# A fused 16-batch transformer and scan kernel: the transfers that stack Q and K's second half, divided by head groups and waited for one batch later

## The reference

```python
x = x + attention(layernorm(x), Wqkv, Wproj)      # 16 heads of 16, rotary, causal softmax
x = x + quant_linear(layernorm(x), weight, bias)  # blocks of 32 rounded to an fp6 grid
x = x + mamba_block(layernorm(x), ...)            # in_proj, conv, scan over 1024 steps, MLP
x = x + quant_linear(layernorm(x), weight, bias)
```

## Time and profile before

| | us |
|---|---|
| median of 3 runs | 10044.25 |
| lowest and highest | 10041.67, 10044.95 |
| profiled execution | 10042.81 |
| its span, first to last instruction | 10040.9 |
| TensorE busy | 7867.1 (78%) |
| VectorE busy | 7696.5 (77%) |
| ScalarE, GpSimd busy | 4309.5, 4340.3 (43% each) |

### The profile page before, as it was taken

One profiled execution on the slowest core, in us unless ns is written; L12 is line 12 of the kernel. 1 busy time (PEld: TensorE's weight loads), 2 busy tenths in 40 slices (PEclk: granted clock), 3 DMA queues, 4 the chain that ended last, 5 costly groups with the idle time before them and its releaser, 6 DMA issues. The chain is left out here.

```text
span 10040.9 us, 98208 instructions
## 1 busy us (share of the span) xinstructions
PE 7867.1 (78%) x31796; PEld 3819.5 (38%) x31796; DVE 7696.5 (77%) x11686; ACT 4309.5 (43%) x8247; POOL 4340.3 (43%) x2663
## 2 busy tenths in 40 slices
PE   5787787787877878787887878778787787877877
PEld 2343343433434334343343433434343343432434
DVE  4787877779687686876868768787787877878777
ACT  2534535354442543525435254353534535345352
POOL 1451714518154171542716336262361724517145
PEclk8898988989889898888989889898898988989889
DMA  3010020200202002020020200102011020100202
GB/s 76 1 38 15 5 48 1 51 1 5 48 0 51 1 9 44 0 51 1 12 40 0 51 1 21 32 0 52 1 28 25 0 52 1 38 15 5 48 0 51
DMA packets 260295, 229.91 MB, mean 23 GB/s; under 512 B 22051, under 2 KB 232739, under 8 KB 259635
## 3 DMA queue, kind: packets, MB, share of 16 engines
q1 hardware_dynamic: 259782, 223.48, 11.6%
HBM read 151.60 MB, written 70.25 MB: 22 GB/s over the span
## 5 line engine op out<-in xcount | busy, mean ns | idle before, releaser
L625 POOL TENSOR_TENSOR arena<-arena 128x1024 f32<-128x1024 f32 x1024 | 2434.3, 2387 | 1330.6 <-DVE arena L1007 879.0
L766 ACT ACTIVATE PS<-arena,Aneg 128x512 f32<-128x512 f32 x2048 | 1410.6, 691 | 1627.2 <-DVE XNT L1047 883.2
L690 ACT ACTIVATE arena<-PS 128x512 f32<-128x512 f32 (+3 forms) x3072 | 1286.8, 509 | 867.0 <-PE PS L1213 861.8
L914 DVE TENSOR_REDUCE pm<-PS 128x1 f32<-128x512 f32 (+3 forms) x1728 | 1050.6, 661 | 336.5 <-PE PS L1192 234.9
L1327 PE MATMUL PS<-XNT,identf 128*128 128x512 f32 x2048 | 1012.1, 618 | 320.0 <-POOL XNT L608 320.0
L587 POOL TENSOR_SCALAR_AFFINE_SELECT arena<-arena 128x512 f32<-128x512 f32 x512 | 328.2, 641 | 2114.5 <-ACT arena L690 2114.5
L1189 PE MATMUL PS<-arena 96*128 96x512 bf16 (+3 forms) x3072 | 1098.0, 382 | 178.8 <-PEq L1411 87.3
L1327 PE MATMUL PS<-arena,identf 128*128 128x512 f32 x2048 | 1025.5, 624 | 161.8 <-DVE arena L1023 161.8
L1213 PE MATMUL PS<-arena 99*128 99x512 bf16 (+3 forms) x3072 | 891.8, 331 | 5.4
L1150 PE MATMUL PS<-identf,arena 128*128 128x128 f32 x1280 | 284.1, 387 | 776.0 <-POOL arena L577 664.6
L1312 PE MATMUL PS<-arena,sel 96*128 96x512 bf16 x1664 | 513.4, 391 | 389.2 <-DVE arena L1023 319.7
(11 more groups left out here) (140 smaller groups left out, 13240.7 us busy)
## 6 DMA issues: line engine op xcount, KB each, us to landing
pieces_scratch<-arena SPq DMA_DIRECT2D x816, 64.0 KB
arena<-pieces_scratch SPq DMA_DIRECT2D x34, 768.0 KB
arena<-pieces_scratch SPq DMA_DIRECT2D x51, 512.0 KB
arena<-pieces_scratch SPq DMA_DIRECT2D x17, 1536.0 KB
arena<-in_x SPq DMA_DIRECT2D x17, 1024.0 KB, 5.6
U<-in_x SPq DMA_DIRECT2D x17, 1024.0 KB, 5.6
arena<-pieces_scratch SPq DMA_DIRECT2D x17, 1024.0 KB
out<-X SPq DMA_DIRECT2D x64, 256.0 KB, 8.3
```

Of the source, the lines that this page charges most:

```text
L625: nc.gpsimd.tensor_tensor(DB[:, n % 2], DTU[:, j, half(th)].unsqueeze(1).to_broadcast([P, SP2, TH]), BB[:, SP2 * sg:SP2 * (sg + 1), :], AL ...
L690: A(PT[s % len(PT)][:, hh, 0:w], bank(t_bank(n))[:, 0:w], ACT.Exp, scale=DH ** -0.5)\
L766: A(bank(da_bank(m)), DT[:, j, half(th)], ACT.Exp, scale=Aneg[:, j, SP2 * sg + ss:SP2 * sg + ss + 1]).then_inc(S("dA"), 1)
L914: V_.tensor_reduce(out=dst, in_=bank(r % 3)[:, 0:share * w].rearrange("p (h w) -> p h w", h=share), op=ALU.max, axis=AX.X, negate=True).th ...
```

## The change

`stack` takes the semaphore that its commands raise. There are four new semaphores, `stacked[0..3]`, one for each group of four heads. K's first half is stacked as before. K's second half and Q are stacked group by group (K, then Q, three commands each), which makes 24 commands out of 6. SP's wait for `pj` stands behind the K commands of group 0. SP no longer waits for these transfers at the end of a pass; PE waits for group g ahead of that group's first score unit in the next pass. In each pass SP, after its twelve maxima commands, waits for each group's semaphore and sets it to zero. The block behind the loop waits for the four as well.

```diff
+        stacked = [ctx.enter_context(nc.semaphore(f"stacked_{g}")) for g in range(NG)]
...
-        def stack(sp, qk, heads, cols):
+        def stack(sp, qk, heads, cols, done):
...
-                  .then_inc(S("stack"), 16)
+                  .then_inc(done, 16)
...
-        N_STACK = 1 + 3 * len(RUNS[0])
+        N_STACK = 1 + len(RUNS[1])
+        N_GROUP = 16 * (len(RUNS[0]) + len(RUNS[1]))
...
-            stack(sp, 1, ALL, half(0))
+            stack(sp, 1, ALL, half(0), S("stack"))
             store_pieces(sp, 2)
             store_pieces(sp, 3)
             sp.wait_ge(S("pcd"), N_PCD * NT // 2)
-            stack(sp, 1, ALL, half(1))
-            if in_loop:
-                sp.wait_ge(S("pj"), NT * 3)
-            stack(sp, 0, ALL, slice(0, T))
+            for g in range(NG):
+                heads = slice(g * HG, (g + 1) * HG)
+                stack(sp, 1, heads, half(1), stacked[g])
+                if in_loop and g == 0:
+                    sp.wait_ge(S("pj"), NT * 3)
+                stack(sp, 0, heads, slice(0, T), stacked[g])
...
+            for g in range(NG):
+                sp.wait_ge(stacked[g], N_GROUP)
+                sp.sem_clear(stacked[g])
             sp.wait_ge(S("dB"), NM)
...
+                    if u % NS1 == 0:
+                        pe.wait_ge(stacked[g], N_GROUP)
                     if r >= 3 and not at:
                         pe.wait_ge(S("red"), r - 2)
...
                 sp.wait_ge(landed, N_OUT)
+                for g in range(NG):
+                    sp.wait_ge(stacked[g], N_GROUP)
```

## The result

| | before | changed |
|---|---|---|
| median, us | 10044.21 | 9967.47 |
| profiled execution, us | 10042.81 | 9965.80 |
| its span, us | 10040.9 | 9963.4 |

The ratio is 0.9924, with a 95% interval of 0.9913 to 0.9936. (The medians are over six runs each; one run of the changed kernel, at a mean granted clock of 0.65, is far above the others and left out of the ratio.)

The account below looks back on a forecast made before the run. SP, waiting for the stack's last bytes, was taken to bound each pass's end; 40.7 + 21.6 - 1.5 = 60.8 us gained gave 9983.4 against 10044.25 (0.61% faster), own range 9976 to 9995, stated range 9974 to 9998.

Parts of the forecast that it names:

- The bound: At a pass's end, SP and behind it the stack's last bytes are the last arrival at the barrier.
- Ahead of the loop: SP leaves after issuing 24 commands, taken as 12 us, at 132.3 instead of 154.0: gain 21.6, range 18 to 26.
- 15 x 2.71: Removing SP's mean end-of-pass wait of 2.71 us at 15 boundaries gains 40.7 us, one for one.
- The check at two boundaries: Boundary waits of 3.9 and 2.3 us: 1.6 more wait, 2.7 longer pass; "the size allows one for one".
- The transfers themselves. Same bytes, same row length: Stack transfers as 24 commands take up to 10% (3.4 us) longer, covered by 20 us: cost nothing.
- The sign that the wait for output would grow to 3.4 us: At the head of each pass, the wait for output grows from 0.7 to about 3.4 us if right.
- I take 0, as the bytes and rows are the same: End of the kernel: one wait falls away, SP's last output wait grows equally; no gain, 0 to 3 lost.
- The added waits: PE's four waits a pass, 64 in all, and SP's waits and clearings cost 1.5 us, range 0.8 to 6.4.
- A: 24 commands hold SP, slower: 10051 at 1.36 us each, turning at 1.33; chance 0.03 above 1.39, 0.04 shared with full B below.
- B: Gain given back behind the barrier to output traffic: 10044, or 10023 if only boundaries fail; in part 0.06, in full within 0.04.
- C: The wait moves from SP to PE, which must wait for group 0; ahead of the loop 9986; chance 0.01.
- The range: Own range 9976 to 9995 from prologue, waits, tail and run-to-run terms; widened to 9974 to 9998 for boundary jitter.

## Why the prediction was wrong, point by point

- **The bound** was read rightly: SP with the stack's last bytes was the last arrival at the barrier, and from SP's last arrival to PE's first load there are 2.3 us in both kernels.
- **Ahead of the loop**: 21.6 forecast, 22.2 measured. SP was held 11.3 us for the 24 commands (12 taken), and PE didn't wait.
- **"15 x 2.71"**, a wait that passes into the time one for one, is the mis-sized term that put the time below the range: 3.39 a pass and 50.9 in all, some 10 of the 16 us missing. The boundary itself gave 2.6 a pass; the other 0.8 came from stages that weren't changed, 1.4 from the attention, where the granted clock falls elsewhere, less 0.6 that the stages behind it took back. The experiments show that lengths of passes don't add up here (0.8 us later at a boundary costs nothing, 1.8 costs 3.4); why they settle where they do stays open. The check at two boundaries gave a warning that was passed over: 1.6 more wait had gone with 2.7 more pass. The pass behind the long wait had another clock than the one before it, at the same place:

```profile
4000.76:4010.76 10.00, 7.85 (x54) 6.44 (x51) 3.46 (x10) 2.77 (x5) 0.27 (x1) 1.00 0.01 2
```

  1.00 where the pass from 3243.77 had 0.83. "The size allows one for one" should have been "it doesn't".
- **"The transfers themselves. Same bytes, same row length"** is the step whose mechanism was wrong. It put a price of 0 to +10% on the division and never asked whether it could be negative, though the rows of before had a hint: 127 GB/s in Q's first command and 200 in its second, at the same row length (the view of the first boundary shows both). The stack became 8 us faster in the mean. In the loop the number didn't suffer by it, as the wait is gone in either way; as far as this step goes, that is luck. The sign that the wait for output would grow to 3.4 us failed by it: that wait is gone. And it was wrong at the end, where "I take 0, as the bytes and rows are the same" stood: behind SP's last command 3.3 us were gained.
- **The added waits** (1.5) can't be found; their cost is below what the passes show.
- **Rivals.** A: 24 commands took 11.3 to 12.9 us, some 0.5 each, far from 1.33. B: the gap behind SP's last command is unchanged, and no output traffic is left by then. C: PE didn't wait for group 0. The cost that the Trainium skill ("DMA: Bandwidth & Descriptors", section "Anatomy of one DMA") gives each transfer, about 2.0 us, overlaps here: 24 commands landed within 24 us at the first boundary, sooner than the six. Its advice in "Measured (HBM→SBUF...)", batches of 1 MiB or more, isn't borne out here: commands of 64 to 384 KB moved at 183 GB/s in the mean, those of 256 to 1536 KB at 139. The page gives both for transfers that GpSimd issues; those here are SP's.
- **The range** was built on bounds of terms that were seen. Some 10 of the 16 us missing come from a term that had no bounds at all, the stages that weren't changed.

## What to carry to other kernels

Before a wait is moved, ask whether the thing waited for can be made faster: here the division alone emptied the wait, and only the unhidden part ahead of the loop needed the move. A division of a transfer into 24 commands took it from 34 us to 26 or to 73 at the same bytes and row lengths, so it belongs in the sum with both signs. Read such a duration at many passes: one boundary had it at 24.0 where the trace has 23.7 to 27.6. In a loop whose passes are bound by TensorE in part, a microsecond saved or added at one end isn't a microsecond of time: look at the granted clock at the same place of the pass in both kernels before a small gain is put down to the edit.

## What the hardware showed that wasn't expected

- A pass stays at 614.4 us with 2.2 us saved or 0.8 us lost ahead of the next pass, and goes to 617.8 with 1.8 lost.
- In the kernels of the table of pass parts, the attention stage takes 144.3 to 144.8 us or 145.9 to 146.7, with the granted clock at 1.00 or 0.83 of full speed in one stretch of 10 us of it, not always the same one.
- Commands over eight partitions used the DMA engines at a share of 0.5 and 60 GB/s; over 16 partitions of 16 heads 1.0 and some 115 GB/s; over 16 to 48 partitions of four heads 183 GB/s in the mean; over 32 partitions of 16 heads 183.
- How long SP is held goes with what is outstanding more than with the number of commands: 24 commands for the same rows took 11.3 to 12.9 us beside 7.2 to 8.5 for six, 24 commands at half of the engines 38 to 47, and six whose Q rows go as packets of 32 KB 3.7 to 4.4.
